# Score maxima of a fused decoder layer taken 17 steps ahead of their scores instead of 13, with their turning and the shift rows moved along

## The reference, cut to what matters

```python
def _softmax(x, axis=-1):
    return jax.nn.softmax(x, axis=axis)
...
scores = jnp.einsum('bhqd,bhkd->bhqk', q, k) * scale
scores = jnp.where(causal[None, None], scores, -jnp.inf)
att = jax.nn.softmax(scores, axis=-1)
y = jnp.einsum('bhqk,bhkd->bhqd', att, v)
...
scores = jnp.einsum('bhqd,bhkd->bhqk', query, key_) / jnp.sqrt(jnp.asarray(DK, dtype=query.dtype))
scores = jnp.where(mask, scores, jnp.asarray(-1000000000.0, dtype=scores.dtype))
attn = jax.nn.softmax(scores, axis=-1)
```

## Time and profile before

| what | us |
|---|---|
| median of the runs | 1254.28 |
| the profiled execution, its own time | 1255.11 |
| its span, first to last instruction | 1253.4 |
| PE busy | 1123.4 (90%) |
| DVE busy | 970.3 (77%) |
| ACT busy | 711.6 (57%) |
| POOL busy | 590.2 (47%) |

### The profile page before, as it was taken

The page is one execution under the profiler, slowest core; times in us unless marked ns, Lnnn a source line. Parts: engine busy times, 40 slices in busy tenths (PEclk is TensorE's granted clock), DMA queues, the critical chain, the costliest instruction groups (busy, mean ns, idle before and its releaser), DMA issues. The chain is left out here.

```text
span 1253.4 us, 21880 instructions
## 1 busy us (share of the span) xinstructions
PE 1123.4 (90%) x7616; PEld 669.1 (53%) x7616; DVE 970.3 (77%) x2636; ACT 711.6 (57%) x1429; POOL 590.2 (47%) x680
## 2 busy tenths in 40 slices
PE   5599999999999999999999999999995218999996
PEld 2355555555555555445454454544342217888895
DVE  6678988888889789888888898988862578676652
ACT  6026555545555656776767777676763104566552
POOL 5666576765868563535353535341123004354523
PEclk9669999999999999999999999999999558999998
DMA  5541534515436345252525252433110605444412
GB/s 174 118 102 36 129 77 101 119 39 132 95 94 144 90 109 128 76 114 73 120 68 120 69 119 88 100 76 78 35 45 25 191 1 162 126 111 110 116 21 34
DMA packets 89329, 117.93 MB, mean 94 GB/s; under 512 B 12065, under 2 KB 59105, under 8 KB 89090
## 3 DMA queue, kind: packets, MB, share of 16 engines
q1 hardware_dynamic: 83074, 107.97, 33.5%
q0 software_dynamic: 6144, 8.52, 4.1%
HBM read 48.63 MB, written 16.91 MB: 52 GB/s over the span
## 5 line engine op out<-in xcount | busy, mean ns | idle before, releaser
L805 ACT ACTIVATE probs<-ps_st 128x512 f32<-128x512 f32 (+3 forms) x1024 | 476.7, 519 | 252.3 <-PE ps_st L638 247.7
L658 PE MATMUL ps_p<-kst,qst 63*128 63x512 f32 (+3 forms) x1024 | 371.6, 428 | 14.8 <-DVE mx L915 13.3
L638 PE MATMUL ps_st<-qst,kst 64*128 64x512 f32 (+3 forms) x1024 | 362.7, 419 | 9.5 <-ACT probs L805 8.5
L913 DVE TENSOR_REDUCE mx<-ps_p 128x1 f32<-128x512 f32 x512 | 325.5, 682 | 58.6 <-PE ps_p L658 58.5
L638 PEld LDWEIGHTS ps_st<-qst,kst 64*128 64x128 f32 x1024 | 166.3, 186 | 264.0 <-ACT probs L805 216.3
L915 DVE CUSTOM_DVE_ANT_0 ps_p<-ps_p,tri 128x128 f32<-128x128 f32 (+3 forms) x512 | 239.3, 514 | 16.2 <-PE ps_p L658 14.3
L619 PE MATMUL ps_o<-probs,vals 128*32 128x512 f32 (+3 forms) x2048 | 232.6, 527 | 0.0
L658 PEld LDWEIGHTS ps_p<-kst,qst 63*128 63x128 f32 x1024 | 169.2, 187 | 29.4 <-DVE mx L915 21.1
L466 POOL TENSOR_SCALAR lnw<-mv 128x4 f32<-128x4 f32 x24 | 5.0, 210 | 282.9 <-DVE mv L899 282.7
L528 POOL TENSOR_SCALAR_AFFINE_SELECT probs<-probs 128x512 f32<-128x512 f32 x128 | 79.5, 635 | 102.8 <-ACT probs L805 102.8
L1224 POOL DMA_INDIRECT out_dram<-moe_part,moe_ids x32 | 58.7, 1834 | 75.4 <-DVE moe_part L1580 69.0
(11 more groups left out here) (232 smaller groups left out, 1930.2 us busy)
## 6 DMA issues: line engine op xcount, KB each, us to landing
qst<-qk_h SPq DMA_DIRECT2D x64, 256.0 KB, 4.7
kst<-qk_h SPq DMA_DIRECT2D x64, 256.0 KB, 5.0
qst<-qk_l SPq DMA_DIRECT2D x32, 256.0 KB, 5.3
kst<-qk_l SPq DMA_DIRECT2D x32, 256.0 KB, 5.2
moe_w1r<-in_w_dram SPq DMA_DIRECT2D x8, 1024.0 KB, 5.1
moe_w2r<-in_w_dram SPq DMA_DIRECT2D x8, 1024.0 KB, 10.0
xin<-in_x_dram SPq DMA_DIRECT2D x8, 512.0 KB, 3.8
xres<-in_x_dram SPq DMA_DIRECT2D x8, 512.0 KB, 4.1
```

Source lines behind the costliest of these rows:

```text
L638: last = nc.tensor.matmul(out, kst[rows, t % 2, pair, kt * P:(kt + 1) * P], qst[rows, t % 2, pair, lo:S], start=True, stop=not masked)
L658: last = nc.tensor.matmul(ps_p1[:, i % 3, 0:keys], qst[rows, t % 2, pair, qt * P:(qt + 1) * P], kst[rows, t % 2, pair, 0:keys], start=True ...
L805: nc.scalar.activation(probs[:, kt, j, 0:n], ps_st[:, i % 2, 0:n], ACT.Exp, scale=float(DH) ** -0.5).then_inc(exp_done, 1)
L913: nc.vector.tensor_reduce(mx[:, g % 2, at:at + 1], bank, AX.X, ALU.max).then_inc(max_done, 1)
```

## The change

`AHEAD` goes from 13 to 17, so each "p1" and its maximum stand four steps earlier in the list. "mt" goes from slot 7 to slot 3, "shift" from slot 9 to slot 5, four steps earlier too. The 16 maxima of a group thus still end five steps ahead of their "mt" (last one at step 16g - 18, "mt" at 16g - 13). Nothing is added or removed, and all buffers are as before.

```diff
-AHEAD = 13
+AHEAD = 17
...
         for n in range(16):
             put(16 * g + n - 16 - AHEAD, "p1", g, n)
-        put(16 * g - 9, "mt", g)
-        put(16 * g - 7, "shift", g)
+        put(16 * g - 13, "mt", g)
+        put(16 * g - 11, "shift", g)
```

## The result

The changed kernel takes 1279.34 us (median of four runs, 1277.82 to 1284.63) beside 1254.01 us before (four runs): ratio 1.0209, 95% interval 1.0188 to 1.0230. It is slower by 25 us; 15.5 us were forecast. Its profiled execution took 1278.59 us, with a span of 1276.8 us (before 1253.4).

The account below looks back on a forecast made before the run. PE's own queue was taken to set the pace; 3.6 + 3.6 (bank waits) + 4.8 + 0.6 (widths) + 3.0 - 0.3 + 0.2 (ends) = 15.5 us on 1255.11 gave 1270.6 us profiled, 1269.8 for the median. Range 1260 to 1278.

Parts of the forecast that it names:

- Where to look: PE's own queue sets the pace; the shift row has 9.1 us of lead, so four more steps are worth nothing.
- point 1: "mt" leaving slot 7 in cross: nothing gained, except 0.25 us in the fourth group, where "lg" follows it.
- Rival A: Taking the lone "mt" out of slot 7 pays: -3 to -4 us, 1251 us; chance 0.06.
- Point 3: Cross, slot 3: third matmul waits for "mt" to leave its bank; 0.60 us six times, 0.72 us five times.
- Point 2: "mt" joining slot 3: 0 where waits hide it, 0.12 us in the third and fourth self group.
- Point 4: New widths of maxima in self attention: 0.8 us a turn in turns 0 to 5, 0.3 each in 6 and 7.
- rival D: PE's clock falls to 1.2 GHz behind half of eleven new stalls in cross: +9 us, 1279 us; chance 0.07.
- Point 5: Ends: four more "p1" ahead of step 0 cost 3.0 us; end -0.3 us; self meeting cross +0.2 us.
- The tail and the meeting of self and cross: Four steps at the end lose their "p1": -0.3 us; four narrow maxima become wide where self meets cross: +0.2 us.
- B: Only the bank waits count, new widths cancel out: 10 us, 1264 us; chance 0.13.
- C: The bank waits are caught up, the start costs 2 us: within 0.2% of before, 1256 us; chance 0.06.
- E: Widths bind harder: 1.2 us a turn and 4 us at the start, 1274 to 1276 us; chance 0.08.

Follow-up runs that it names:

- e7: Kernel before with the maxima 11 steps ahead instead of 13, units renumbered so each slot keeps its width, "mt" and "shift" unmoved: 1253.57 us, 0.9975.
- e1: Changed kernel with "mt" and "shift" put back to slots 7 and 9, maxima still 17 steps ahead: 1273.62 us, 1.0158.
- e3: Changed kernel with its units renumbered so every slot has the width of maximum it had before: 1263.69 us, 1.0078.
- e5: Changed kernel with "mt" as the last entry of its step instead of the first: 1281.51 us, 1.0189.
- e10: Kernel before plus 36 spare full-height matmuls ahead of "p1" in slots 7 to 9, third and fourth groups of turns 0 to 5: 1277.86 us, 1.0188.
- e12: Kernel before plus 36 spare row-halved matmuls in slots 7 to 9, third and fourth groups of turns 0 to 5: 1255.88 us, 1.0015.
- e2: Changed kernel with an edit meant to put "mt" last in its step, which left the order unchanged: 1280.51 us, 1.0205.

## Why the prediction was wrong

The forecast was 1269.8 us, its range 1260 to 1278; the result, 1279.34, lies above it. The side was right, with a chance of 0.88 for slower.

- **Where to look, and point 1: right for cross.** "mt" leaving slot 7 gains nothing there: slot 8's "st" is still released by ACT (748.00). The lead is worth nothing by itself, and 11 steps are enough (e7). Rival A falls in cross. In self attention point 1 said nothing, and there "mt" out of slot 7 does give 0.40 us back in the second group, once the widths are the new ones (13.44 us in e1, 13.04 in the changed kernel); with the old widths it is 0.06 (12.97 before, 12.91 in e3).
- **Point 3, the bank waits: right**, in place and nearly in size. Predicted 0.60 and 0.72 us, measured 0.65 and 0.80; in sum 7.8 us for 7.2. e5 shows that the wait is the cause: with "mt" behind the others 0.1 to 0.2 us stay in these groups.
- **Point 2: right in being small.** e5's remainder of 0.1 to 0.2 us in cross is the price of "mt" where nothing hides it; in these groups I had set it at nothing.
- **Point 4, the waits by width: right in sum, not in place.** 0.8 us a turn was predicted, 0.73 measured, but 0.30 of it in the first group, which I had set at 0 (12.76 to 13.06 us), 0.07 in the second, 0.16 and 0.20 in the third and fourth. That the sum fits is luck: it holds the 0.40 us that "mt" gave back in the second group, of which the prediction knew nothing.
- **Point 4 is also the step that failed**: "Sum 0.8 us a turn, in turns 0 to 5: 4.8 us; turns 6 and 7 ... 0.3 each" has no term for the clock. Turns 0 to 7 got 14.3 us longer, not 5.4. The eight drops of turns 0 to 5 cost 8 times 1.05 = 8.4 us (13.86 and 13.92 us for groups of 12.83 and 12.86; the rest of the 12.8 is 6 times 0.73). The ninth stands in the fourth group of turn 6, of 13.68 us, which in e1, without a drop, takes 12.15. Together some 10 us, and the miss is 9.5 us between the medians. In the profiled pair it is 7.9 (23.4 us of span for 15.5): there the drop that turn 14 lost takes 1.2 off, and the other terms together came out 0.8 us under the forecast. The profile of before showed what a drop costs, though the 1.7 us that I took from it are more than the 1.05 us of a self group. I used it in rival D alone, and there for the bank waits in cross, where the changed kernel has no drop at all. That D's 1279 us is the time measured is luck: its place is wrong. Its counter-argument, that stalls of 0.3 to 0.9 us stand in many places at full clock, holds for cross; for the stalls that I had myself put at slots 7 to 9, ahead of a "qk", I never asked.
- **Point 5, the start: open within its spread.** +1.8 us in the profiled pair for 3.0 predicted. But the first "st" starts at 77.8, 75.7 and 74.5 us in three executions of the same start (before, e10, e12), and at 79.4 to 80.8 in the nine with a lead of 17: 4 us apart by their means. The tail and the meeting of self and cross: turns 14 and 15 are 0.3 us shorter, two bank waits of 1.2 us included and a lost drop of 1.2 us (14.92 to 13.74 us in its group); turn 7 is 0.9 us shorter: its third group, where PE waited 1.22 us at the `If` before, takes 12.08 us instead of 13.93, and the first two, with the `If` now at the end of the second, 1.15 us more. Neither was resolved further.

Of the rivals, B and C named too little. E's price of harder widths was not needed.

## What to carry to other kernels

When a change makes TensorE wait in many equal places, ask there for the clock too: price the wait and, beside it, the same stretch at 1.2 GHz, by a row that shows one. A reorder that keeps every count can cost twice, by a shared bank's queue and by a new rhythm of widths, and one run for each part, with its counterpart in the kernel before, tells them apart. When entries share few banks, look for each at the one whose bank it takes over. Putting the entry with the late consumer last freed 0.5 and 0.7 us in the cross groups here, and cost 0.5 us in a self group, where another entry then had to wait.

## What the runs showed of the hardware

- The clock fell with PE recorded as busy throughout (16.48 of 16.48 us in e10), so the busy share of the profile does not tell whether the clock is safe. Drops came behind three waits of PE of 0.1 to 0.2 us each, 0.42 in sum (changed kernel, 270.77 to 272.06), and behind three full-height matmuls between row-halved ones without any recorded wait (e10).
- Spare row-halved matmuls of 512 columns, three in each of twelve groups, cost nothing measurable there (12.67 us with and without), where the same number of full height cost 1.1 us a group even without a drop (13.78 against 12.67).
- Which groups have a drop differs from one execution to the next of the same program (the changed kernel and e2), and so does its time: 1277.5 to 1284.6 us over both. Their number follows the recorded waits (table above). Why some groups with the same waits have one and others not is open.
